# A new order of the attention steps, rows normalised by ScalarE from a kept scale and shift, and statistics taken a step ahead

## The reference

```python
x = x + tanh(g_xattn[0]) * attention0(layernorm(x), ctx)      # 16 heads of 16, causal
x = x + tanh(g_ffn[0])   * experts0(layernorm(x))             # 16 experts, top 2, plus a shared expert
x = x + tanh(g_xattn[1]) * attention1(layernorm(x), ctx)      # 16 heads of 16, queries masked
x = x + tanh(g_ffn[1])   * experts1(layernorm(x))             # 8 experts, top 2
```

## Time and profile before

| | |
|---|---|
| median of 3 runs | 956.94 us (954.53 to 961.73) |
| profiled execution, its own time | 956.38 us |
| its span | 954.5 us |
| TensorE busy | 750.8 us (79%) |
| VectorE busy | 595.5 us (62%) |
| ScalarE busy | 385.9 us (40%) |
| GpSimd busy | 331.7 us (35%) |
| granted TensorE clock, mean | 0.886 |

### The profile page before, as it was taken

The page is one execution under the profiler, slowest core; times in us unless marked ns, Lnnn a source line. Parts: engine busy times, 40 slices in busy tenths (PEclk is TensorE's granted clock), DMA queues, the critical chain, the costliest instruction groups (busy, mean ns, idle before and its releaser), DMA issues.

```text
span 954.5 us, 28657 instructions
## 1 busy us (share of the span) xinstructions
PE 750.8 (79%) x10036; PEld 619.2 (65%) x10049; DVE 595.5 (62%) x1567; ACT 385.9 (40%) x907; POOL 331.7 (35%) x371
## 2 busy tenths in 40 slices
PE   7999898898577997777878777741599999999700
PEld 4767676666466885556656566541599999999700
DVE  4668877786566667477886877774444544544433
ACT  2444444344235663244443343432354445445200
POOL 0124334344440222256646566555100000000075
PEclk8999998898879998999987888765799999999955
DMA  4241222221333554143323324211411111111144
GB/s 143 68 145 55 62 76 63 69 79 45 100 103 103 173 184 153 44 128 111 113 98 99 125 85 138 74 60 62 144 47 54 45 44 49 49 44 34 34 132 132
DMA packets 50616, 85.17 MB, mean 89 GB/s; under 512 B 7920, under 2 KB 37744, under 8 KB 50288
## 3 DMA queue, kind: packets, MB, share of 16 engines
q1 hardware_dynamic: 40304, 55.34, 18.9%
q0 software_dynamic: 9664, 28.32, 9.0%
q10 hardware_dynamic: 576, 0.52, 0.2%
HBM read 55.84 MB, written 28.31 MB: 88 GB/s over the span
## 4 chain that ended last, share of the span: by engine, by line
PE 27%; POOL 12%; issue 10%; DVE 6%; DMA 4%; ACT 1%; POOLq 0%; SPq 0%; DVEq 0%; ACTq 0%
PE bank L1518 11%; PE bank L1543 11%; POOL arena L540 4%; POOL work L622 3%; POOL xg L565 2%; POOL work L548 2%; DVE work L849 1%; DMA work<-in_ctxT 1%; POOL rstd L533 1%; DVE work L868 1%; PE bank L1506 1%; PE bank L1353 1%; DVE x L906 1%; DMA work<-in_slab 1%; PE bank L1283 1%
## 5 line engine op out<-in xcount | busy, mean ns | idle before, releaser
L1518 PE MATMUL bank<-work,arena 128*128 128x128 bf16 x2496 | 198.5, 220 | 0.0
L1543 PE MATMUL bank<-arena,work 128*128 x1104 | 178.5, 273 | 3.6 <-DVE work L1195 2.4
L1518 PEld LDWEIGHTS bank<-work,arena 128*128 x2496 | 166.9, 98 | 6.1
L572 POOL DMA_DIRECT2D y<-work x44 | 31.6, 718 | 288.3 <-DVE work L1182 218.0
L533 POOL TENSOR_TENSOR rstd<-vareps,mhalf 128x1 f32<-128x1 f32 x64 | 37.6, 587 | 257.3 <-DVE vareps L832 257.3
L849 DVE TENSOR_REDUCE work<-bank 128x4 f32<-128x512 f32 x128 | 79.4, 682 | 37.5 <-PE bank L1290 21.4
L1543 PEld LDWEIGHTS bank<-arena,work 128*128 128x128 bf16 x1104 | 92.8, 98 | 9.3 <-issue 4.2
L540 POOL TENSOR_TENSOR arena<-work,arena 128x384 bf16<-128x384 f32 (+3 forms) x64 | 97.6, 1533 | 0.7
L711 ACT ACTIVATE arena<-work 128x384 bf16<-128x384 f32 (+3 forms) x64 | 50.9, 795 | 107.1 <-DMA work<-in_slab 107.1
L799 ACT ACTIVATE work<-bank,b 128x128 f32<-128x128 f32 x160 | 45.6, 368 | 110.9 <-PE bank L1518 110.9
L1216 DVE TENSOR_TENSOR work<-work 128x1024 bf16<-128x1024 f32 x40 | 49.0, 1225 | 62.3 <-ACT work L805 62.3
(11 more groups left out here) (157 smaller groups left out, 1543.0 us busy)
## 6 DMA issues: line engine op xcount, KB each, us to landing
work<-in_slab SPq DMA_DIRECT2D x32, 512.0 KB, 3.9
work<-xg SPq DMA_DIRECT2D x88, 128.0 KB, 2.1
y<-work POOLq DMA_DIRECT2D x44, 256.0 KB, 2.5
work<-in_slab SPq DMA_DIRECT2D x32, 192.0 KB, 2.4
xg<-zeros SPq DMA_DIRECT2D x36, 128.0 KB, 2.5
work<-in_ctxT SPq DMA_DIRECT2D x32, 128.0 KB, 3.3
x<-in_x SPq DMA_DIRECT2D x16, 128.0 KB, 2.6
wat<-in_wat SPq DMA_DIRECT2D x8, 256.0 KB, 5.4
```

Of the source, the lines that this page charges most:

```text
L1518: i = pe.matmul(to, column(w, c, e, most, P), v, start=(k == 0 and q == 0), stop=(k == KT - 1 and q == 2))
L1543: i = pe.matmul(bank[6 + j.par][:, 0:D], a, column(w, c, e, most, D), start=(k == 0 and q == 0), stop=(k == nk - 1 and q == 2))
```

## The change

The two engines' orders in the attention stage are rewritten, all steps are written out (no loop), and LAG is 3.

- `moments(0, ·)` is taken for tile t+3 instead of t+2, `moments(1, ·)` for t-1 instead of t-2. VectorE no longer normalises: it makes one number a row, `shift` = -mean * scale (new L879). ScalarE applies `x * scale + shift` a step later (`normalise`, one ACTIVATE of 128x256 for each tile).
- `power` writes the scale of the second norm straight into `kept_rstd`; the copy L841 is gone.
- On TensorE `proj_o(t-1)` comes before `proj_k(t+2)` instead of last; on VectorE `residual(t-1)` comes before `combine`, which is now for t+3, and both `moments`.
- On GpSimd the two `power` come after `fetch` (now t+4) and `split_lo(t, 0)`, not before them.
- `slot_pair` has room for two pairs, so its writer waits for the pair before the last.
- The parts of `choose` are spread: part 0 in odd steps, part 1 in even steps, 2 and 3 at the end of odd steps. The last tile is weighed and divided in step 15, and the tail's pieces of routing and shared expert are laid out anew.

```diff
-LAG = 4
-PEEL = (7, 7)
+LAG = 3
...
-        slot_pair = sb("slot_pair", [P, 2, 2], I32)
+        slot_pair = sb("slot_pair", [P, 2, 4], I32)
...
+            def power(w, L, t):
+                n = t.plus(T * L)
                 need(pool, ve_ok[w], n.v + 1)
-                pool.tensor_tensor(rstd[w][:], vareps[w][:], mhalf[:], ALU.pow).then_inc(rstd_ok[w], 1)
+                pool.tensor_tensor(scale_of(w, t)[0], vareps[w][:], mhalf[:], ALU.pow).then_inc(rstd_ok[w], 1)
...
-                    if inside(t, 2):
-                        power(0, t.plus(T * L + 2))
-                    if inside(t, -2):
-                        power(1, t.plus(T * L - 2))
-                    for k in rows_at(t)[:1]:
+                    for k in rows[:1]:
                         low_rows(L, k)
-                    if L and inside(t, 3):
-                        fetch(t.plus(3))
+                    if L and inside(t, 4):
+                        fetch(t.plus(4))
                     if inside(t, 0):
                         split_lo(L, t, 0)
+                    if inside(t, 3):
+                        power(0, L, t.plus(3))
+                    if inside(t, -1):
+                        power(1, L, t.plus(-1))
...
+            def normalise(w, L, t):
+                n = t.plus(T * L)
+                need(act, shift_ok[w], n.v + 1)
+                need(act, pe_T[w], n.v - 1)
+                scale, bias = scale_of(w, t)
+                act.activation(xn[2 * w + t.par], at(x, t.v), ACT.Identity, scale=scale, bias=bias).then_inc(xn_ok[w], 1)
...
+            def shift(w, L, t):
+                n = t.plus(T * L)
+                scale, bias = scale_of(w, t)
                 need(dve, rstd_ok[w], n.v + 1)
+                dve.tensor_scalar(bias, meanvar[w][:, 0:1], scale, -1.0, ALU.mult, ALU.mult).then_inc(shift_ok[w], 1)
...
+                    if inside(t, -1):
                         residual(L, t.plus(-1))
+                    if L and inside(t, 3):
+                        combine(0, t.plus(3))
+                    if inside(t, 3):
+                        moments(0, L, t.plus(3), loaded(t.plus(3)))
+                    if inside(t, -1):
+                        moments(1, L, t.plus(-1), (x_ok, t.v + T * L))
```

More of the change, by code:

```diff
@@ L195, in tiles @@
         gate.trips = trips
-    with eng.Fori(0, trips) as r:
-        for i in range(unroll):
-            step(Tile(r, first + i, unroll))
+    if trips:
+        with eng.Fori(0, trips) as r:
+            for i in range(unroll):
+                step(Tile(r, first + i, unroll))
     if gate:
@@ L948, in choose @@
+                    link(dve.tensor_tensor(tmp, logits_, over_e(m[:, part, :]), ALU.is_equal))
+                    link(dve.tensor_tensor(tmp, tmp, revs, ALU.mult))
+                    link(dve.tensor_reduce(r, tmp, AX.X, ALU.max))
+                    link(dve.tensor_tensor(oh[:, part], over_e(r), revs, ALU.is_equal))
                     if part == 0:
-                        step(6, dve.scalar_tensor_tensor(out=rest, in0=oh[:, 0], scalar=-3e38, in1=pair, op0=ALU.mult, op1=ALU.add))
+                        link(dve.scalar_tensor_tensor(out=rest, in0=oh[:, 0], scalar=-3e38, in1=pair, op0=ALU.mult, op1=ALU.add))
@@ L957, in choose @@
-                    if inside(t, 5):
-                        need(dve, pe_o, n.v + 6)
-                    step(12, dve.tensor_tensor(rank, bank[7][:, D + 32:D + 32 + 2 * E].rearrange("p (t e) -> p t e", t=2),
-                                               taken[:, 0:E].unsqueeze(1).to_broadcast([P, 2, E]), ALU.add))
+                    link(dve.tensor_tensor(rank, bank[7][:, D + 32:D + 32 + 2 * E].rearrange("p (t e) -> p t e", t=2),
+                                           taken[:, 0:E].unsqueeze(1).to_broadcast([P, 2, E]), ALU.add))
@@ L1036, in _, with last @@
                     queries(t0)
+                    combine(0, Tile(0, 2))
+                moments(0, L, Tile(0, 2), loaded(Tile(0, 2)))
+                shift(0, L, Tile(0, 2))
                 def attend(t, L=L, loaded=loaded):
-                    even = t.off % 2 == 0
+                    def last(k, *parts):
+                        for part in parts:
+                            choose(L, Tile(0, k), part)
                     if inside(t, 0):
                         scores(L, t)
-                    if inside(t, -1):
+                    if inside(t, -1) and t.v < T:
                         divide(L, t.plus(-1))
@@ new lines, in attend @@
+                    if inside(t, -1):
+                        moments(1, L, t.plus(-1), (x_ok, t.v + T * L))
+                    if L == 0 and t.v == T:
+                        shared(pair_of(0))
+                    if t.v < T:
+                        if t.v % 2 and t.v >= 5:
+                            last(t.v - 5, 0)
+                        if t.v % 2 == 0 and t.v >= 6:
+                            last(t.v - 6, 1)
+                    if inside(t, 3):
+                        shift(0, L, t.plus(3))
@@ L1458, in attend @@
                         proj_v(L, t.plus(1))
+                    if L == 0 and v == T:
+                        for q in pair_of(0):
+                            shared(q)
+                    if inside(t, -1):
+                        bank7_read(L, v - 1, max(0, v - 3), max(0, (v - 6) // 2))
+                        proj_o(L, t.plus(-1))
                     if inside(t, 2):
@@ L1481, in attend @@
-                    if inside(t, -1):
-                        proj_o(L, t.plus(-1))
-                    if L == 0 and step_is(t, T + 1, T + 2, T + 3):
-                        shared(pair_at(t)[1])
-                tiles(pe, T + LAG, *PEEL, attend)
+                    if v == T - 1:
+                        weigh_v(L, t)
+                    if inside(t, -1):
+                        need(pe, x_ok, v + T * L)
+                    if v % 2 and 7 <= v < T:
+                        rank(L, t.plus(-7))
@@ L1488, in _ @@
+                tiles(pe, T + LAG, T + LAG, 0, attend)
                 if L == 0:
```

267 lines of the change are left out of this document (139 added, 128 removed).

## The result

The changed kernel takes **983.47 us** (median of 4 runs, 983.24 to 988.07) against 955.74 for the kernel before beside it: ratio **1.0289** [1.0235, 1.0343]. It is slower by 27.7 us. The forecast was 954 with a range up to 976, so the time lies outside it, on the side of rival (c), but not for all of that rival's reasons.

A forecast was written before the change was run, and what follows sets the result against it. Layer 0's attention was taken as close to TensorE's own work, layer 1's as set by an engine-to-engine chain. From 956.4: +27 (layer 1's steps), -4 (layer 0's steps), -14 and -11 (tails) gave 954 us, range 930 to 976.

The forecast's parts named there:

- rival (c): Layer 1's loop through GpSimd with all its waits, matmuls at 1.2 GHz, smaller tail gains: 978 us, chance 0.22.
- The chain residual, combine, fetch, slab half, roots, shift: Layer 1, steps 1 to 11: new loop through GpSimd sets the step, 15.8 us without scatter, against 13.4 before.
- Its sum, +17: Layer 1, steps 1 to 6: +14 us for the loop through GpSimd and +3 for the lower clock.
- 0.5 us a step: Layer 1, steps 1 to 6: added for the chain's matmuls running part of the time at 1.2 GHz, +3 us.
- 96 was forecast: Layer 1, steps 7 to 11: 19.2 us a step, with scatter, held small operation and 1.0 for the clock.
- Step 12 has no fetch any more and takes about 14.5: Layer 1, step 12: without a fetch the step takes about 14.5 us; steps 7 to 12 together +11.
- Steps 13 and 14, with no fetch and no statistics ahead, 26.5: Layer 1, steps 13 and 14: 26.5 us against 30.5 before, -4.
- 13.2, and up to 1 of port waits: 14.0: Layer 0's steps: the wait for `proj_o` plus VectorE's remaining work, 14.0 us a step against 14.8; sum -4.
- Layer 0's -14: Layer 0's tail: -6 us from an earlier first shared tile, -8 from landing waits removed by the second pair.
- Layer 1's -11: Layer 1's tail: last residual at about 17 us, then seven tiles of 3.4; 43 against 53.8.
- rival (e): Layer 1, steps 1 to 6: VectorE's shift is held by the slab half too, 13 us more, 967; chance 0.04.
- layer 1's start, +3: Layer 1's start: a third combine, moments and shift ahead of the first maxima and one more gather, +3 us.

The follow-up runs named there:

- the filled kernel: Changed kernel with ten 128x512 matmuls on zeros ahead of the transpose of the maxima in layer 1: 983.13 us, ratio 1.0301.
- seventh: Changed kernel with combine and tile t+3's statistics ahead of the residual, and GpSimd waiting for the maxima's small operations before the second slab half: 921.10 us.
- ninth: Changed kernel with GpSimd's wait for the small operations and, in layer 1, only the fetch moved behind both roots: 938.50 us, ratio 0.9744.
- tenth: Changed kernel with combine and statistics ahead of the residual, GpSimd's wait for the small operations, and the fetch behind the roots: 921.13 us, ratio 0.9567.
- eighth run: Changed kernel with the rows normalised by VectorE again, ahead of the residual, instead of by ScalarE: 984.74 us, ratio 1.0231.

## Why the prediction was wrong, by its own steps

**Layer 1, steps 1 to 6: the mechanism was right.** The chain residual, combine, fetch, slab half, roots, shift was forecast at 15.8 us a step, and the filled kernel has it at 15.66. Its sum, +17, is what was measured (97.6 against 80.7), but by two errors that cancel. The clock was put at 0.5 us a step and costs 1.4: the prediction spread the slow time over the step, while it falls on TensorE's own part of the chain, right after its wait (`proj_v` 2.08 against 1.10 us). The first of the six steps took 11.9 us, since counted from score to score the loop first shows in the second.

**Layer 1, steps 7 to 11: right.** 96 was forecast, 95.4 measured, with the held operations as the reason, 9.2 us in all (none in step 7, 1.8 to 3.1 in the others) for the 1.7 to 2.0 a step that were forecast.

**Layer 1, steps 12 to 14: the first step that failed.** "Step 12 has no fetch any more and takes about 14.5. [...] Steps 13 and 14, with no fetch and no statistics ahead, 26.5": 41.0 forecast, 57.8 measured. The fetch is gone, but the scatter remains, and behind it the two slab halves with the low rows between them. The prediction let one small operation be held by one slab half, 1.7 to 2.0 us. In fact both are held, one after the other, 5.2, 3.7 and 5.1 us from step 12 on by the two lines' times. That is 14.0 of the 16.8 us that were missed; the kernel with the wait on GpSimd has these three steps at 43.5 us.

**Layer 0's steps: the second.** "13.2, and up to 1 of port waits: 14.0", -4 in sum; measured +5.6. Steps 7 to 12, from which the term was worked out, came near it (85.3 us, 14.2 a step); what failed was what the prediction took for the other steps. Steps 13 and 14 took 30.0 us against 24.7, where up to 2 more was allowed, and steps 0 to 6 took 88.3 against 84.2, where 1 less was forecast.

The holds of the two small operations are 14.5 us over the layer, with 2.7 each in steps 10, 12 and 14, and these three steps are 16.6 to 16.7 us long, in part at 1.2 GHz. That the slab half is only 0.97 us here was taken as harmless, but three GpSimd instructions in a row hold both operations. Without these holds steps 7 to 14 are 11.5 to 13.2 us, below the 14.0.

In steps 0 to 6 the two small operations were held for 0.3 us only. Step 6 was 16.1 us: ahead of its maxima L979, an operation of `choose`, took 3.03 us beside GpSimd's L626, which splits the shared expert's weights (128x1536, 3.11 us). In all seven other variants in which that operation was held so, step 6 took 14.5 to 17.4 us, and in the three in which it was not (the seventh, ninth and tenth runs) 11.6 to 11.7. In step 3 VectorE waited 1.14 us for a tile of x to land and TensorE 1.92 us for a block of ctxT; no run looked into that step.

**The tails: sign right, size not.** Layer 0's -14 was -9.0: the first shared tile began 14.8 us after the score and not 11 (17.3 before), and no gain of it is seen, for with one pair the way to layer 1 is 7.3 us longer than before; the second pair, put at 8, is worth 20 in this order and more than makes up for that. Layer 1's -11 was -6.1: the last residual came 21.5 us after the score where 17 was worked out, with 3.8 us of held operations in between in that step; the scatters then followed at 3.2 us each, as forecast (3.4).

**Right and small:** ScalarE's two added operations cost nothing (eighth run); the 128x1 shift is not held, so rival (e) falls (12 of its 64 ran beside a slab half, none took more than 0.22 us); layer 1's start, +3, was +2.2. **Not foreseen:** the kernel's start was 3.0 us shorter and layer 0's experts 3.4. The start is scatter: in the ten kernels built on the changed one it took 18.3 to 22.1 us, against 17.5 here and 20.5 before. No run looked into the experts.

**The rivals.** (c), slower at 978 by low clock in the matmuls, was right on the clock, and its tails, -9 and -6, are what was measured. It decides "from 17.5 us a step in steps 1 to 6"; the five full ones took 17.1 to 17.4. The result went beyond it by what it didn't have either, the double holds.

In sum the forecast of -2 was 29 us short of the +27.0 of the spans: layer 1's last three steps 16.8, layer 0's steps 9.6 and the tails 9.9 make 36.3; the start (-3.0), the first expert stage (-3.4) and layer 1's steps 0 and 7 to 11 (-1.4) give most of the rest back.

## What to carry to other kernels

In an engine's queue, ask of each instruction that is put ahead of another not only what it waits for, but what its own end releases: the fetch ahead of the roots cost 4.2 us a step, while the slab half moved behind them cost as much, through a load and two engines. Where VectorE's short operations sit on the critical chain, look at which GpSimd tensor instructions can be running at that moment, count the ones in a row and not only the longest, and hold GpSimd back by a semaphore if need be (28.7 us here for one line). And where the part of a chain that runs on TensorE comes right behind its idle time, its durations are to be taken from rows at 1.2 GHz, not from a mean clock of the stage.

## What the hardware showed that was not expected

- A VectorE operation that GpSimd holds is not let in between two GpSimd instructions that follow without a gap: L893 stood still for 4.22 us, over two slab halves of 2.1 us.
- With the low rows (L564) between two slab halves, one operation gets through and the next is held again: 2.87 and 2.65 us.
- GpSimd's issue of an indirect DMA holds no such operation by itself: L889 took 0.17 us beside it in three steps (beside L575 in two, beside the gather L558 in one). But where a slab half followed, L889 stood from 0.70 us ahead of that instruction's recorded start (602.38 and 603.08) to its end.
- The scalar_tensor_tensor of 128x16 with two inputs in SBUF is held like the tensor_scalar (2.67 us at most). The tensor_scalar of 128x1 wasn't: none of L879's 64 took more than 0.22 us, and 12 of them ran beside a slab half, all in its first 0.5 us.
